# The router's sum from float32r halves of the turned x, with the weight stationary, and the normalization's chain at the head of step 1

## The reference, cut to what matters

```python
# x, ctx: (16, 256, 2048) = (batch, channel, time); 8 heads of 32 channels, window of 16
q = Wq @ layernorm(x) + bq ; k = Wk @ ctx + bk ; v = Wv @ ctx + bv
dots[b,h,t,w] = sum_d q[b,h,d,t] * k_padded[b,h,d,t+w] * 32**-0.5
o = einsum('bhtw,bhdtw->bhdt', softmax(dots), v_window)
x = x + tanh(g_xattn) * (Wo @ o + bo)            # "x1" below
h = layernorm(x)                                  # over time, 2048 values a row
logits = h @ router_weight.T + router_bias        # (4096 rows, 64 experts)
w_dense = softmax(logits), kept at the 8 largest, 0 elsewhere
x = x + tanh(g_ffn) * (h * w_dense.sum(-1) + w_dense @ expert_bias)   # everything in float32
```

## Time and profile before

| | before |
|---|---|
| median of 3 runs | 1546.06 us (1544.34 to 1550.62) |
| profiled execution, its own time | 1549.06 us |
| its span | 1547.0 us |
| TensorE granted clock, mean | 0.974 |
| busy: PE / DVE / ACT / POOL | 94% / 80% / 75% / 75% |
| L1225, router matmuls, busy | 130.1 us in 1024 records |
| L908 turn, idle before it | 68.0 us, of which 67.4 for POOL's L495 |

### The profile page before, as it was taken

The page is one execution under the profiler, slowest core; times in us unless marked ns, Lnnn a source line. Parts: engine busy times, 40 slices in busy tenths (PEclk is TensorE's granted clock), DMA queues, the critical chain, the costliest instruction groups (busy, mean ns, idle before and its releaser), DMA issues.

```text
span 1547.0 us, 66674 instructions
## 1 busy us (share of the span) xinstructions
PE 1457.9 (94%) x28162; PEld 1196.4 (77%) x28162; DVE 1232.8 (80%) x2938; ACT 1156.2 (75%) x2025; POOL 1160.6 (75%) x1126
## 2 busy tenths in 40 slices
PE   4799999999999999999999999999999999999986
PEld 3577877878887888888788888878888887778764
DVE  5477887878888787888888788888878888787774
ACT  3588877778787877888787787878778787767652
POOL 4587777788777878778787887878788787677661
PEclk9799999999999999999999999999999999999896
DMA  7454455554545555454555545455554545434232
GB/s 231 122 127 107 127 149 140 145 161 113 162 131 140 144 154 162 112 161 133 140 144 154 162 114 162 131 140 147 152 161 114 160 133 140 123 82 134 57 77 90
DMA packets 365576, 210.39 MB, mean 136 GB/s; under 512 B 294496, under 2 KB 295520, under 8 KB 361056
## 3 DMA queue, kind: packets, MB, share of 16 engines
q1 hardware_dynamic: 365280, 206.14, 49.1%
HBM read 136.88 MB, written 33.55 MB: 110 GB/s over the span
## 4 chain that ended last, share of the span: by engine, by line
PE 60%; DVE 19%; issue 6%; ACT 6%; POOL 5%; DMA 2%; SPq 1%; POOLq 0%; ACTq 0%; DVEq 0%
PE ps_j L1123 26%; PE ps_s L1183 9%; PE ps_a L1148 7%; PE ps_r L1225 6%; PE ps_s L1123 5%; DVE prob_t L908 4%; DVE st_x L915 2%; PE ps_s L1178 2%; POOL prob L495 2%; PE ps_a L1202 2%; PE ps_t L1165 1%; PE ps_a L1203 1%; DMA x_in<-x_dram 1%; DVE st_in L820 1%; DVE nt_x L814 1%
## 5 line engine op out<-in xcount | busy, mean ns | idle before, releaser
L488 POOL TENSOR_TENSOR score<-score,p_inv 128x384 f32<-128x384 f32 x256 | 219.2, 856 | 110.5 <-DVE p_inv L902 107.6
L495 POOL TENSOR_TENSOR prob<-score,prob 128x384 f16<-128x384 f32 x256 | 262.6, 1026 | 32.8 <-ACT prob L660 31.6
L1183 PEld LDWEIGHTS ps_s<-kv_win,q_col 32*32 32x32 f32 x16384 | 197.2, 106 | 59.2 <-issue 58.7
L1183 PE MATMUL ps_s<-kv_win,q_col 32*32 32x48 f32 x16384 | 233.8, 205 | 4.0 <-issue 3.8
L908 DVE STREAM_TRANSPOSE prob_t<-prob 128x512 f32<-128x512 f32 x256 | 177.1, 701 | 68.0 <-POOL prob L495 67.4
L469 POOL TENSOR_TENSOR c_lo<-c_in,c_hi 128x1024 fp32r<-128x1024 f32 x64 | 152.7, 2385 | 91.0 <-ACT c_hi L634 91.0
L1148 PEld LDWEIGHTS ps_a<-prob_t,v_diag 128*128 128x128 f16 x6528 | 175.8, 98 | 51.0 <-DVE prob_t L908 34.0
L1148 PE MATMUL ps_a<-prob_t,v_diag 128*128 128x48 f16 (+2 forms) x6528 | 188.3, 183 | 26.9 <-DVE prob_t L908 20.2
L464 POOL TENSOR_TENSOR att_lo<-att,att_hi 128x512 fp32r<-128x512 f32 x128 | 161.7, 1275 | 50.1 <-ACT att_hi L620 48.8
L598 ACT ACTIVATE kv_win<-ps_j,v_bias 128x512 f16<-128x512 f32 x128 | 108.2, 847 | 104.0 <-PE ps_j L1123 104.0
L1123 PE MATMUL ps_j<-c_hi,wkv_hi 128*128 128x512 f32 x512 | 172.5, 419 | 14.1 <-POOL c_lo L469 7.0
(11 more groups left out here) (149 smaller groups left out, 3320.0 us busy)
## 6 DMA issues: line engine op xcount, KB each, us to landing
v_diag<-v_turn SPq DMA_DIRECT2D x512, 68.0 KB
c_in<-ctx_dram SPq DMA_DIRECT2D x64, 512.0 KB, 4.9
x_in<-x_dram SPq DMA_DIRECT2D x64, 512.0 KB, 5.7
x_res<-x_dram SPq DMA_DIRECT2D x64, 512.0 KB, 4.7
out_dram<-x SPq DMA_DIRECT2D x32, 1024.0 KB, 8.0
c_sq<-ctx_dram SPq DMA_DIRECT2D x60, 512.0 KB, 5.6
x<-ctx_dram SPq DMA_DIRECT2D x4, 512.0 KB, 7.0
x<-experts_dram SPq DMA_DIRECT2D x2, 512.0 KB, 10.2
```

The costliest lines, as they stand in the source:

```text
L488: pool.tensor_tensor(score[:, u], score[:, u], p_inv[:, u, :].unsqueeze(2).to_broadcast([P, HALF, KEYS]), ALU.mult).then_inc(pm_rdy, 1)
L495: pool.tensor_tensor(part(prob[:, u % 2], 1)[:, :, 0:KEYS], score[:, u], part(prob[:, u % 2], 0)[:, :, 0:KEYS], ALU.subtract).then_inc(pl_ ...
L1183: ins = pe.matmul(s[head(h), n * KEYS:(n + 1) * KEYS], q_col[head(h), g, at:at + SUB], kv_win[c % 2][head(h), 0, g, at:at + KEYS], start=F ...
```

## The change

The turned x is now split: ScalarE writes its float32r half `turn_hi`, VectorE the remainder `turn_lo` (`turned_low`). The weight is split once into two halves of 64 columns, side by side in `wr_both`, and is the stationary operand: four pairs of float32r instructions a step, each with 256 moving columns (both groups at once), sum in `ps_r` with the experts on partitions, high half below, low half above. Once a batch, in step 1, ScalarE copies the sum to `acc` (`logit_sums`), and four float32 matmuls with the identity turn it back and add the halves (`fold_logits`). TensorE's `rows` of the other group, `router` and the square's matmul wait for `turned_low` too.

The room for the two new tiles comes from `c_sq`, which becomes a part of `v_turn`, and `wr`, which is staged in x1. So the load of `c_sq` waits for the step's v_diag copies, and `values_turn` for the square. On VectorE the normalization's chain of x1 moves from the end of step 0 into step 1, cut in pieces around turn(2) and turn(3); `stats_in` and `values_turn` move behind `largest(0)` and `shift(0)`.

```diff
-        c_sq = sb("c_sq", [P, G, CHUNK])
...
+        c_sq = v_turn[:, :, 0:CHUNK]
...
-        x1_t = sb("x1_t", [P, G, TB, P])
-        wr = sb("wr", [P, T // P, E])
+        turn_hi = sb("turn_hi", [P, G, TB, P], F32R)
+        turn_lo = sb("turn_lo", [P, G, TB, P], F32R)
+        wr_staged = x1[1][:, 1, 0:(T // P) * E].rearrange("p (n e) -> p n e", e=E)
+        wr_both = sb("wr_both", [P, T // P, 2 * E], F32R)
...
+        acc = lg[:].rearrange("p g j e -> p g (j e)")
...
                     need(sp, sq_rdy, nth(b, c, 7))
-                    sp.dma_start(c_sq[:], rows_in).then_inc(sq_ld, 16)
+                    if live(b, c, 0):
+                        for g in range(G):
+                            need(sp, vd_ld[g], nth(b, c, 0) * (16 * HPG))
+                    sp.dma_start(c_sq, rows_in).then_inc(sq_ld, 16)
...
+                if b == 0 and c == 1:
+                    pool.wait_ge(wrh_rdy, 1)
+                    pool.tensor_tensor(wr_both[:, :, E:2 * E], wr_staged, wr_both[:, :, 0:E], ALU.subtract).then_inc(wrl_rdy, 1)
...
-                    act.activation(x1_t[:, g], ps_t[:].rearrange("p (k t) -> p k t", k=TB), ACT.Copy).then_inc(xt_rdy[g], 1)
+                    act.activation(turn_hi[:, g], ps_t[:].rearrange("p (k t) -> p k t", k=TB), ACT.Copy).then_inc(xt_rdy[g], 1)
+
+                def logit_sums():
+
+                    need(act, r_mm, nth(b, c, -2))
+                    need(act, wd_rdy, 2 * (b - 1))
+                    act.activation(acc, ps_r[:, 0:G * P].rearrange("p (g c) -> p g c", g=G), ACT.Copy).then_inc(acc_rdy, 1)
...
+                if c == 1 and seq(b - 1):
+                    logit_sums()
                 if now:
                     exponent(0)
+                if b == 0 and c == 0:
+                    act.wait_ge(r_ld, 16 * 4)
+                    act.activation(wr_both[:, :, 0:E], wr_staged, ACT.Copy).then_inc(wrh_rdy, 1)
...
+                def turned_low(g):
+
+                    need(dve, xt_rdy[g], nth(b, c, -2))
+                    need(dve, r_mm, nth(b, c, -3))
+                    dve.tensor_tensor(turn_lo[:, g], ps_t[:].rearrange("p (k t) -> p k t", k=TB), turn_hi[:, g],
+                                      ALU.subtract).then_inc(xtl_rdy[g], 1)
+
                 def values_turn(g):
 
                     need(dve, halo_r, nth(b, c, 0))
+                    need(dve, sq_rdy, min(nth(b, c, 7), N))
                     need(dve, vd_ld[g], nth(b, c, -1) * (16 * HPG))
                     dve.transpose(v_turn[:, g], kv_win[c % 2][:, 1, g]).then_inc(vt_rdy[g], 1)
...
+                if stats:
+                    ch, db = place(c, 4)
+                if live(b, c, -2):
+                    turned_low(0)
+                if routing:
+
+                    need(dve, st2_rdy, b * (NCH * G))
+                    dve.memset(pad[:, 2:3], 0.0).then_inc(aggr2, 1)
+                    for g in range(G):
+                        dve.bn_aggr(mv_x1[:, g], st_x1[:, g]).then_inc(aggr2, 1)
+                    need(dve, aggr2, b * (G + 1))
+                    root_seed(root2, (b - 1) * ROOT, mv_x1, var_x1, half_x1, rs_x1, neg_mean_x1)
                 if before:
                     turn(2, -1)
+                if routing:
+                    root_steps(root2, (b - 1) * ROOT, half_x1, nt_x1, rs_x1, ln2_rdy, range(1))
+                if before:
                     turn(3, -1)
-                if stats:
-
-                    ch, db = place(c, 4)
+                if routing:
+                    root_steps(root2, (b - 1) * ROOT, half_x1, nt_x1, rs_x1, ln2_rdy, range(1, 3))
+                if stats and not routing:
+
                     need(dve, x_ld[ch], (b + db + 1) * 16)
                     stats_in(1, ch)
+                if live(b, c, -2):
+                    turned_low(1)
+                if now:
+                    largest(0)
+                    shift(0)
+                if stats and not routing:
                     stats_in(0, ch)
-                if now:
-                    largest(0)
+                if stats and routing:
+                    need(dve, x_ld[ch], (b + db + 1) * 16)
+                    stats_in(1, ch)
+                if now:
                     values_turn(0)
                     values_turn(1)
-                    shift(0)
                 if stats and c == 3:
...
+                if stats and routing:
+                    stats_in(0, ch)
...
-                if c == 0 and seq(b - 1):
-
-                    need(dve, st2_rdy, b * (NCH * G))
-                    dve.memset(pad[:, 2:3], 0.0).then_inc(aggr2, 1)
-                    for g in range(G):
-                        dve.bn_aggr(mv_x1[:, g], st_x1[:, g]).then_inc(aggr2, 1)
-                    need(dve, aggr2, b * (G + 1))
-                    inverse_root(root2, (b - 1) * ROOT, mv_x1, var_x1, half_x1, nt_x1, rs_x1, neg_mean_x1, ln2_rdy)
...
-                    need(dve, r_mm, (b - 1) * NCH + NCH)
+                    need(dve, fo_mm, b)
...
                     need(pe, xt_rdy[1 - g], nth(b, c, -2))
+                    need(pe, xtl_rdy[1 - g], nth(b, c, -2))
...
                     need(pe, xt_rdy[1], nth(b, c, -2))
+                    need(pe, xtl_rdy[1], nth(b, c, -2))
                     if ch == 0:
                         need(pe, lg_rdy, b * G)
                         if b == 0:
                             need(pe, sum_rdy, 2)
+                            need(pe, wrl_rdy, 1)
                     for k in range(TB):
-                        for g in range(G):
-                            ins = pe.matmul(ps_r[:, g * E:(g + 1) * E], x1_t[:, g, k], wr[:, ch * TB + k],
-                                            start=(ch == 0 and k == 0 and g == 0),
-                                            stop=(ch == NCH - 1 and k == TB - 1), skip_group_check=True)
+                        for n, v in enumerate((turn_hi, turn_lo)):
+                            ins = pe.matmul(ps_r[:, 0:G * P].rearrange("p (g c) -> p g c", g=G),
+                                            wr_both[:, ch * TB + k], v[:, :, k],
+                                            start=(ch == 0 and k == 0 and n == 0),
+                                            stop=(ch == NCH - 1 and k == TB - 1 and n == 1))
                     ins.then_inc(r_mm, 1)
+
+                def fold_logits():
+
+                    need(pe, acc_rdy, b)
+                    for g in range(G):
+                        for i in range(2):
+                            ins = pe.matmul(ps_r[:, g * E:(g + 1) * E], acc[:, g], ident[:, i * E:(i + 1) * E],
+                                            start=(g == 0 and i == 0), stop=(g == G - 1 and i == 1), skip_group_check=True)
+                    ins.then_inc(fo_mm, 1)
...
+                if c == 1 and seq(b - 1):
+                    fold_logits()
```

31 lines of the change are left out of this document (20 added, 11 removed).

## The result

The changed kernel takes 1659.41 us (median of 4 runs, 1656.11 to 1661.22) against 1548.34 us for the kernel before (4 runs, 1544.34 to 1553.49): ratio 1.0713, 95% interval 1.0674 to 1.0752. It is 111 us slower. I had forecast 1632, with a range of 1585 to 1655; the direction and the main cause hold, but the time lies above the range.

What follows compares the result with a forecast made beforehand. TensorE, 94% busy, was taken as the bound. From 1549.06 us, steps 1 +112 less 7, steps 0 -11, steps 2 -14, steps 3 +3, batches 14 and 15 +1 each, start +1: +86, 1635; 1632 against the median, range 1585 to 1655.

Steps and rivals of the forecast that it cites:

- Router's block: Router matmuls on TensorE, every step: 8 instructions at 0.115 us take 0.92 instead of 1.83, 0.9 saved.
- The fold: Once a batch, in step 1: four float32 instructions take 0.9 us on TensorE, giving back the router's saving there.
- The chain that opens step 1: VectorE's x1 normalization, held by GpSimd's products: attend(1) starts at T + 8.45 instead of 4.73, TensorE idle 4.1 us.
- The clock: After step 1's idle time TensorE falls to 1.2 GHz in about 11.5 of 13 batches, 4.56 us; step 1 +8.6.
- Steps 0, 2 and 3: The other steps of each batch: -0.75, -0.9 and +0.2 us a step, -11, -14 and +3 in all.
- Step 2: Third step of a batch: gains 0.9 us from the shorter router, -14 over 16 steps.
- Step 3: Last step of a batch: gains nothing, ScalarE waits for the input's normalization chain, 0.2 us later; +3 over 14 steps.
- Step 0: First step of a batch: gains 0.9 less 0.15, so 0.75 us, -11 over 15 steps.
- Chain free: Rival, step 1: c_lo begins late, the chain runs through, VectorE is late; about 0 a batch, 1548 us; chance 0.08.
- faster: Rival: chain free in step 1 and VectorE's lag taken up in step 2's slack; 1526 us; chance 0.12.
- Clock stays: Rival, step 1: the chain is held but TensorE keeps 2.4 GHz; +45, 1591 us beside the runs' median; chance 0.10.
- c_sq in v_turn: c_sq's load waits for the v_diag copies: hidden, in slow cases up to 3 us late in step 1.

Runs made afterwards that it cites:

- e1: The changed kernel with x1's whole normalization chain at the head of VectorE's step 1, ahead of turned_low(0): 1599.43 us.
- e2: The changed kernel in its own order, but x1's chain rounds keep their intermediate in PSUM, so none reads two SBUF tensors: 1597.32 us.
- e6: The changed kernel, x1's chain rounds in PSUM, aggregate, seed and first round ahead of turned_low(0), and step 2's last two router-weight stages behind turned_low(0): 1559.14 us.
- e12: The kernel before with 9 router matmuls a step instead of 16, leaving out three quarters of the second group's router sum: 1536.16 us.
- e14: The kernel before with e13's edits of step 3 and of SyncE's load order, without anything of the change: 1520.85 us.
- e11: The kernel before with only c_sq placed in v_turn's columns and the two waits this adds: 1547.02 us.
- e13: e6 with step 3's last input statistics and normalization chain moved earlier, its rounds in PSUM, and x_in's load ahead of x_res's: 1527.19 us.
- e15: e13 with x_in's load also ahead of the load of c_sq: 1509.99 us.

## Why the prediction was right in its cause and short in its size

**Router's block.** The pace was right, the block a little short. Its instructions start 0.12 apart, but the first stands 0.20 ahead of the second, and 1.03 us pass in TensorE's row until the next block, in batch 8's step 0:

```profile
834.34 0.36 PE L1282 MATMUL ps_r<-turn_hi,wr_both 128*128 128x256 f32 x1
834.54 0.28 PE L1282 MATMUL ps_r<-turn_lo,wr_both 128*128 128x256 f32 x1
...
835.37 0.34 PE L1233 MATMUL ps_s<-mask,ident_b 128*128 128x384 bf16 x1
```

The old block takes 1.81 in the same count, and 1.73 in steps 2. So 0.8 is saved, 0.7 in steps 2, and not 0.9. In batch 8's step 1, at the lower clock, the instructions start 0.21 apart. The fold takes 0.91 at full clock: right.

**The chain that opens step 1.** Right in nearly every part: the two held instructions (2.30 and 1.18 us), their neighbours, turn(3), attend(1) at T + 8.38 where I had 8.45, the idle time 4.05 for 4.1. That three batches pay at L1355 instead I hadn't seen. e1 and e2 show it by two ways, 60 and 62 us of the 111.

**The clock.** The term of the sum that was too large. I took batch 14, with 10 us at the lower level and 4.56 us lost, for the size of all. The kernel before has a second case, which I had not read, in batch 15: there the clock is low for 10 us behind a wait of only 2.43 us, and attend(1) to the next step takes 21.17.

```profile
1445.49 2.10 PE L1148 MATMUL ps_a<-prob_t,v_diag 128*128 128x32 f16 x51 [2.43 <-DVE prob_t L908]
```

It gives the same size, so it would not have mended the term; but it shows that a wait shorter than the 3.07 us at which the clock stayed can bring it down. In the kernel after, the stretch of batch 8 lasts 6.8 us, so that attend(1) to the next step takes 19.55 and step 1 is +6.5 instead of +8.6. Why the stretches are shorter there is open. Together with batches 14 and 15 the forecast had +107 for the steps 1, and they came to +84.

**Steps 0, 2 and 3: the step that failed.** I wrote that a microsecond taken from TensorE's row is worth a microsecond, as long as the other engines keep their order, and booked -0.75, -0.9 and +0.2 a step: -22 in all. Measured, over all steps of a kind: -0.8, +7.7 and +19.4, so +26. That is 48 us too little, against 23 too much in the steps 1 (107 less 84); head and tail cancel. 86 + 48 - 23 is the 111 measured. These stand behind the 48, beside the router's block that saves 0.1 to 0.2 less a step:

- Step 2: I had turned_low(0) at T + 1.9 in every step. In step 2 VectorE stands in the router's weights until T + 3.0, L1149 held for 1.03 us beside GpSimd's product (0.29 us at its shortest); rows(1) waits 0.99. e6 gives it back, 0.95 a step.
- Step 3, delay: I had seen that it gains nothing, since ScalarE waits for the chain, and booked 0.2 for the chain's own delay. That term was too small. The chain ended at T + 10.6 to 10.8 and now ends at 11.2 in seven of 13 batches and at 11.7 to 12.1 in six. values(0) follows it, at 16.64 in the seven and 17.1 to 18.4 in the six, for 16.1 to 16.2 before, and a step without a low clock takes 24.5 and 25.0 to 25.4 for 24.0. That is 10 of the 18 us by which these 13 steps are longer.
- Step 3, clock: time that TensorE gains ahead of a wait that ends late is not just lost, since the wait grows. At values(0) it was never above 0.8 us in these batches before and is up to 2.04 now. In five of 13 batches the clock falls and the step takes over 26 us, the other 7 to 8 us: with waits of 1.82, 2.04 and 2.04 at values(0), with one of 1.41 behind an issue gap of 1.09, and once behind an issue gap of 1.47. e12, in which the chain is untouched, has the same growth of the wait and four such steps.
- Step 0: shorter at best by 0.55 (20.36 for 20.91: the router's 0.78, less the 0.2 by which it starts later), but in the mean by 0.17, since gaps which the profile calls issue are longer after: 9.7 and 9.6 us at attend and at scores against 5.2 and 3.8. What makes them was not found; they differ between kernels whose TensorE orders are the same (5.2 at attend before, none in e14).

The tail, for which I had booked 0: in the last batch, where nothing covers them, TensorE waits 2.15 and 2.13 us for turn_lo and runs the fold at the lower clock in 1.97.

**Rivals.** "Chain free" and "faster" were excluded by one row, L840 at 2.30. "Clock stays" fails too: the shortest of the 13 steps 1 is 26.84, and T + 8.4 with the usual 16.88 behind it, less 0.8 and plus 0.9, would be 25.4. But a fourth case, that TensorE's gain is worth nothing, was missing, and e12 is the run that a rival should have named: 51 us for 10.

**c_sq in v_turn** and the casts: hidden, right for this kernel (e11). It is no property of the alias: e13, which needs x_in's load earlier, pays for the queue behind it, and e15, with that load ahead of c_sq's, is 17 us faster.
